# Node numbers in PSUM as bfloat16, written by a TensorE turn, for the 0/1 matrices of a graph layer

## What is computed

```python
h = (x_flat @ W_gat).reshape(M, HEADS, NUM_EXPERTS)
a_src = (h * att_src).sum(-1)
a_dst = (h * att_dst).sum(-1)
e = jax.nn.leaky_relu(a_src[src] + a_dst[dst], negative_slope=0.2)
e_max = jax.ops.segment_max(e, dst, num_segments=M)
ee = jnp.exp(e - e_max[dst])
denom = jax.ops.segment_sum(ee, dst, num_segments=M)
...
agg = jax.ops.segment_sum(msg, dst, num_segments=M).reshape(M, HEADS * NUM_EXPERTS) + b_gat
...
out = out + g[..., None] * (hh @ W2[ei] + b2[ei])
```

## Time and profile before

| | us |
|---|---|
| three runs: median (lowest to highest) | 1598.84 (1597.82 to 1599.68) |
| span of the profiled execution | 1598.4 |
| DVE busy | 1248.3 |
| POOL busy | 876.9 |
| PE busy | 869.5 |
| ACT busy | 451.1 |

### The profile page before, as it was taken

The page is one execution under the profiler, slowest core; times in us unless marked ns, Lnnn a source line. Parts: engine busy times, 40 slices in busy tenths (PEclk is TensorE's granted clock), DMA queues, the critical chain, the costliest instruction groups (busy, mean ns, idle before and its releaser), DMA issues.

```text
span 1598.4 us, 36932 instructions
## 1 busy us (share of the span) xinstructions
PE 869.5 (54%) x13361; PEld 683.8 (43%) x13361; DVE 1248.3 (78%) x2794; ACT 451.1 (28%) x813; POOL 876.9 (55%) x891
## 2 busy tenths in 40 slices
PE   0323233248888862554488884666666665553340
PEld 0223222237777752554133332555555555543340
DVE  6998898876667644996999986677777667788878
ACT  0232242224444433773133330212211121121120
POOL 0045665546666660000577777777777777777700
PEclk9999855556766655776699995555555555555555
DMA  7000000022222216100310110111111111111101
GB/s 166 7 20 21 27 28 27 29 56 50 51 49 49 50 51 95 42 28 12 29 10 10 10 10 10 12 12 12 12 14 12 13 12 12 12 12 24 23 2 26
DMA packets 113952, 45.80 MB, mean 29 GB/s; under 512 B 92631, under 2 KB 108799, under 8 KB 113538
## 3 DMA queue, kind: packets, MB, share of 16 engines
q1 hardware_dynamic: 84098, 22.43, 7.3%
q0 software_dynamic: 27632, 19.12, 7.0%
q10 hardware_dynamic: 2064, 2.10, 0.7%
HBM read 28.17 MB, written 15.93 MB: 28 GB/s over the span
## 4 chain that ended last, share of the span: by engine, by line
DVE 36%; issue 8%; PE 8%; DVEq 1%; ACT 0%; ACTq 0%
DVE edges_work L1950 7%; PE edges_acc L2460 3%; DVE edges_hotT L1950 3%; PE edges_acc L2449 2%; DVE all_stack L2195 1%; DVE graph_left L1823 1%; DVE graph_left L1821 1%; DVE all_eo L1992 1%; DVE all_sums L2211 1%; DVE edges_left L1821 1%; DVE edges_left L1823 1%; DVE graph_left L2274 1%; DVE edges_high L2244 1%; DVE all_sums L2271 1%; DVE edges_term_parts L1820 1%
## 5 line engine op out<-in xcount | busy, mean ns | idle before, releaser
L336 POOL DMA_INDIRECT edges_rows<-table,edges_src x576 | 563.0, 978 | 175.5 <-issue 174.9
L192 DVE TENSOR_TENSOR sorting_keys<-sorting_keys 128x512 f32<-128x512 f32 (+2 forms) x370 | 209.8, 608 | 16.6 <-ACT sorting_keys L317 13.2
L723 POOL DMA_INDIRECT x_rows<-mixture_sent,mixture_slot x128 | 144.3, 1128 | 127.5 <-DVE mixture_slot L785 89.0
L728 POOL DMA_INDIRECT y_rows<-mixture_yt,mixture_xin x144 | 156.2, 1085 | 103.6 <-ACT mixture_yt L950 79.4
L2508 ACT ACTIVATE edges_hotT<-edges_h 128x1024 bf16<-128x1024 bf16 x72 | 69.8, 1021 | 326.1 <-PE edges_h L2403 326.1
L1063 PE MATMUL mixture_bank<-mixture_xT,sorting_w_part 128*128 128x128 bf16 x864 | 111.9, 260 | 30.7 <-ACT mixture_xT L936 14.3
L1063 PEld LDWEIGHTS mixture_bank<-mixture_xT,sorting_w_part 128*128 x864 | 86.9, 107 | 57.4 <-issue 45.4
L1950 DVE TENSOR_TENSOR edges_work<-edges_feats,all_eo 128x2048 bf16<-128x2048 f32 x48 | 109.3, 2277 | 0.2 <-DVE all_eo L2003 0.2
L2460 PE MATMUL edges_acc<-edges_term_parts,edges_work 128*128 128x20 bf16 x1728 | 51.6, 179 | 100.6 <-DVE edges_term_parts L1824 100.6
L2460 PEld LDWEIGHTS edges_acc<-edges_term_parts,edges_work 128*128 128x128 bf16 x1728 | 49.1, 104 | 108.1 <-issue 108.1
L2403 PE MATMUL edges_h<-edges_ident,edges_work 128*128 128x128 bf16 x576 | 67.2, 310 | 31.7 <-DVE edges_work L1950 31.7
(11 more groups left out here) (477 smaller groups left out, 2170.0 us busy)
## 6 DMA issues: line engine op xcount, KB each, us to landing
edges_rows<-table,edges_src POOLq DMA_INDIRECT x576, 2.4
mixture_xin<-x_rows SPq DMA_DIRECT2D x144, 49.0 KB, 1.8
all_eo<-y_rows SPq DMA_DIRECT2D x16, 256.0 KB, 3.9
y_rows<-mixture_yt,mixture_xin POOLq DMA_INDIRECT x144, 2.6
sorting_w<-in_L_ffn_w_dram SPq DMA_DIRECT2D x4, 512.0 KB, 8.4
x_rows<-mixture_sent,mixture_slot POOLq DMA_INDIRECT x128, 2.3
out_dram<-all_x_sb SPq DMA_DIRECT2D x8, 256.0 KB
constants_src_i<-in_L_ffn_edge_index_dram SPq DMA_DIRECT2D x1, 1024.0 KB, 5.2
```

Of the source, the lines that this page charges most:

```text
L192: self.st.mark(dve.tensor_tensor(target[half], source[0], source[1], (ALU.min, ALU.max)[half]))
L336: pool.indirect_dma_start(to, None, rows, where).then_inc(done, 16)
L723: pool.indirect_dma_start(x_rows, bass.IndirectOffsetOnAxis(ap=slot[g % 2][:, c, t:t + 1], axis=0), now[c][:, t, :], None).then_inc(scatte ...
L728: pool.indirect_dma_start(y_rows, bass.IndirectOffsetOnAxis(ap=xin[j % XB][:, ROWX - 2:ROWX - 1].bitcast(U32), axis=0), yt[j % YB][:, :], ...
```

## The change

A third row of integers is written by POOL: `own_i`, in which every column of partition p holds p. DVE turns it to bfloat16 (`own16`). PE turns `own16` (a transpose with `ident16`) and writes the result as bfloat16 to 64 words of the bank of `node_ps`, beside the float32 numbers. The result is again the row 0 to 127 in each partition: `node_ps16`. The three calls of `equal_to` read `node_ps16` in place of `node_ps`; the float32 numbers stay for the stray edges. `ident16` is made earlier. PE waits for `own16` and `ident16`, and DVE waits for the turn before it writes `node_ps`.

```diff
+        own_i = a.sb("own_i", [P, P], I32)
+        own16 = a.sb("own16", [P, P], BF16)
...
+        node_ps16 = node_ps[:, P:P + P // 2].bitcast(BF16)
...
+        own_ready = a.sem("own_numbers_ready")
+        own_turned = a.sem("own_numbers_turned")
...
             pool.iota(node_i[:, :], pattern=[[1, P]], base=0, channel_multiplier=0).then_inc(numbered, 1)
+            pool.iota(own_i[:, :], pattern=[[0, P]], base=0, channel_multiplier=1).then_inc(numbered, 1)
...
-            spare = pool.alloc_register("pool_spare_edges"), numbered, 2
+            spare = pool.alloc_register("pool_spare_edges"), numbered, 3
...
-            dve.wait_ge(numbered, 2)
+            dve.wait_ge(numbered, 3)
             st.mark(dve.tensor_copy(block_f[:, :], part_i[:, :]))
+            st.mark(dve.tensor_copy(ident16[:, :], ident[:, :]))
+            st.link(dve.tensor_copy(own16[:, :], own_i[:, :]))
+            dve.sem_inc(own_ready, 1)
...
             def one_hot(s, u, g):
-                equal_to(hot[s % 4], node_ps, P, local16[:, u, tiles(g), :]).then_inc(hot_ready, 1)
+                equal_to(hot[s % 4], node_ps16, P, local16[:, u, tiles(g), :]).then_inc(hot_ready, 1)
...
-                equal_to(hot_last[at], node_ps, P, n16).then_inc(last_made, 1)
-                equal_to(hot_block[at], node_ps, T, b16).then_inc(last_ready, 1)
+                equal_to(hot_last[at], node_ps16, P, n16).then_inc(last_made, 1)
+                equal_to(hot_block[at], node_ps16, T, b16).then_inc(last_ready, 1)
...
-            st.mark(dve.tensor_copy(ident16[:, :], ident[:, :]))
             st.mark(dve.memset(one16[:, :], 1.0))
...
             st.link(dve.tensor_copy(node16[:, :], node_i[:, :]))
+            dve.wait_ge(own_turned, 1)
             st.mark(dve.tensor_copy(node_ps[:, 0:P], node16[:, :]))
...
             pe.wait_ge(node_steps, marks["feats"])
             turn_keys(0)
+            pe.wait_ge(own_ready, 1)
+            pe.transpose(node_ps16, own16[:, :], ident16[:, :]).then_inc(own_turned, 1)
             pe.wait_ge(at_ready, 2)
```

## The result

| | before | changed kernel |
|---|---|---|
| median of four runs each (lowest to highest), us | 1598.33 (1596.63 to 1599.68) | 1568.27 (1567.63 to 1570.0) |
| span of the profiled execution, us | 1598.4 | 1568.2 |
| DVE busy, us | 1248.3 | 1131.8 |
| POOL busy, us | 876.9 | 879.2 |
| PE busy, us | 869.5 | 861.8 |

The ratio is 0.9816, with a 95% interval of 0.9802 to 0.983: 30.1 us less. The prediction had 1568 and a range of 1564 to 1576. DVE was relieved of 1248.3 - 1131.8 = 116.5 us and the kernel became 30 us shorter; the difference is the subject of what follows.

The account below looks back on a forecast made before the run. DVE with its partners was taken to set the end, the gathers 31.0 us under it. 31.0 + 1.1 (last step's shorter begin) - 1.0 (longer gathers) = 31.1; span 1598.4 to 1567.3, plus 0.4, rounded to 1568 us; range 1564 to 1576.

Parts of the forecast that it names:

- The pace: DVE's comparison matrices: two elements per cycle with two-byte PSUM numbers, 2277 to 1210 ns for large, 1210 to 677 for small.
- Rival A: DVE's matrices: PSUM sets the pace, so they stay at 2277 ns and the time is 1599.2 us; 8 in 100.
- The start stage: Before the gathers: the new cast and wait make DVE's chain 0.35 us later; gathers still start at 775.0.
- The expert stage: DVE bounds it, PE would be next: a group falls from 11.11 to 9.96 us, 17.3 us over 15 groups.
- the late pairs: Two late pairs of matrices, on a chain of DVE and PE alone: 2 x 1.60 = 3.2 us gained.
- The edge steps: Each step gains 0.63 us, not 1.07, since DVE then waits for PE; 12.6 us up to step 20.
- Rival B: Edge steps: PE holds them and the earlier matrix gains nothing, 1577.6 us, or 1570 with a third; 8 in 100.
- The waits on gathers: DVE waits on gathers about 9 us at step 20 and some 3 us at the last step.
- The cap of 31.0: At the last step: gathers land 31.0 us before DVE begins it, so DVE's gain is cut to 31.0.
- longer gathers: Last lap: more of DVE's two-source work falls under the gathers and stretches some, an estimated loss of 1.0 us.
- Rival C: POOL's gathers: the faster form holds POOL one for one, adding 138 us, so 1706 us; 4 in 100.
- deciding point: Rival C decides the time from 31 us added to the gathers, 0.22 us for each us of matrices.

Follow-up runs that it names:

- experiment 4: Changed kernel, but each edge's number is read once with step 0 in the innermost dimension instead of from two copies side by side; 1598.66 us, ratio 1.0003.
- experiment 1: Changed kernel with all added parts kept, but the three `equal_to` calls read the float32 numbers; 1598.83 us, ratio 1.0 to the kernel before.
- experiment 10: The changed kernel again, unaltered, on the same chip as the others; 1569.71 us, ratio 0.9815 to the kernel before.
- experiment 2: Changed kernel, but the edge steps' matrices read the float32 numbers, so only the expert stage has the change; 1576.07 us, ratio 0.9857.
- experiment 3: Changed kernel, but the expert stage's matrices read the float32 numbers, so only the edge steps have the change; 1574.88 us, ratio 0.9851.
- experiment 6: Changed kernel with the last of the 16 gathers of each step left out, 36 of 576; 1550.85 us, ratio 0.971 to the kernel before.
- experiment 9: Changed kernel with the third set of source numbers placed at the second lap's last step, not its ninth (step 23, not 20); 1569.08 us, ratio 0.9814.
- experiment 8: Changed kernel with the start stage's second product made behind the table rows and the stray edges' gather issued after step 3's gathers; 1566.69 us, ratio 0.9805.
- experiment 11: Changed kernel with the edits of experiments 8 and 9 together; 1567.87 us, ratio 0.9807 to the kernel before.
- experiment 5: Changed kernel, but the three `equal_to` calls read the bfloat16 numbers in SBUF instead of PSUM; 1612.17 us, ratio 1.0093 to the kernel before.

## Why the prediction was right

**The pace.** 1210 and 677 ns were forecast; 1212 to 1217 and 678 were measured. Rival A, the old pace, is excluded for this form, and with it the rule of the Trainium skill's page "VectorE: DVE Perf Modes", section "The perf-mode tier table", that was cited for it: one element per cycle for any two-tensor operation with a PSUM operand. 2048 elements in 1212 ns contradict it. The prediction's own working rests on the width alone and has no term for the doubled copies of the edges' numbers; experiment 4 shows that without them the pace and the time of A come out.

**The start stage.** 0.35 us of cost was forecast. From the last copy of the rows for the table to the cast into PSUM, DVE took 6.38 us and now takes 6.70; experiments 1 and 10 have 6.71. Before, and then now:

```profile
763.64 0.29 DVE L1907 COPY edges_rows<-edges_as_sb 128x256 f32<-128x256 f32 x1
...
770.02 0.29 DVE L1982 CAST edges_feats<-edges_node 128x128 f32<-128x128 bf16 x1
```

```profile
762.74 0.29 DVE L1913 COPY edges_rows<-edges_as_sb 128x256 f32<-128x256 f32 x1
...
769.44 0.29 DVE L1991 CAST edges_feats<-edges_node 128x128 f32<-128x128 bf16 x1
```

That is 0.32 us. By the first matrix it is 0.6 (776.61 - 762.74 in place of 776.92 - 763.64), because two of DVE's operations beside the first gathers take 0.77 and 0.70 us where they took 0.56. The profiled execution also has all of the graph layer 0.9 us earlier (first gather at 774.1, has 775.0). This isn't the change's: the copy shown is already 0.9 us earlier, and it stands ahead of the first new instruction.

**The expert stage, a term sized too low.** 11.11 us per group were to become 9.96. Measured on one line of PE's timeline, the second layer of the networks:

```profile
851.20 1.07 PE L2328 MATMUL edges_acc<-edges_work,edges_u 128*64 128x512 f32 x2
...
861.12 1.07 PE L2328 MATMUL edges_acc<-edges_work,edges_u 128*64 128x512 f32 x2
```

It is 9.92 us. But the prediction counted the 15 groups behind the first and gave the first nothing. In the first group PE also waited for matrices: in the kernel before this line begins at 786.0 and begins for the last time at 956.5; in the changed kernel at 782.7 and 935.3. So 3.3 us are won as it begins, 0.9 of them the shift, and 21.2 at its end. Where 17.3 - 0.35 = 16.95 us were forecast, 20.3 came out: the first group's share was put at nothing without a reason. With the late pairs the first `raw` is at 975.77 and not 1001.46: 25.7 us, 24.8 without the shift, and 21.2 were forecast. Experiment 2 agrees: 22.5 us at the end, where the same terms of the prediction gave 20.2, its 1.07 for the first matrix of the edge steps left out.

**The edge steps.** 0.63 us per step were forecast. In the first lap the steps alternate between 13.28 and 13.54 us, a mean of 13.41, where before they were 14.03: 0.62. The wait of DVE for PE ahead of `found` came as described: 18.0 us over 36 steps, of which the last step has 1.6, as before. Rival B, no gain in the edge steps, is excluded by experiment 3 alone: 23.6 us.

**The waits on gathers.** Both stand where they were forecast. The one at step 20 is 13.0 us and not 9: the 3.6 us more that the expert stage gave are in it. The last one is 4.1 us and not 3: the last gather's rows came later than the sum had them. Experiments 2, 3, 6 and 9 show that these waits are the cap itself.

**The sum.** The cap of 31.0 less 1.0 for longer gathers puts DVE's last step at 1516.9; it begins at 1517.76, 0.8 us later. The last gather starts 0.3 us later than before though the first started 0.9 earlier, so the chain is 1.2 us longer, where 1.0 was estimated. And the last rows are there 3.9 us behind the start of the last gather, where the sum had the median landing of 2.4; in experiments 8 to 11 it is 2.6 to 3.7. The step's end then takes 1568.2 - 1517.8 = 50.4 us, as forecast; in experiments 2, 3 and 6, whose last step doesn't wait, it takes 51.5 as before. So the 3.6 us by which the expert stage was underrated don't show in the time: the cap absorbs them, and a forecast whose first term was off by a sixth still came out.

Part of the closeness is luck. The 1.0 us of longer gathers came out in size but not where it was looked for, in the last lap. The gathers of the two traces by the stretch in which they were issued, with POOL's time in them:

| | gathers | before, us | now, us |
|---|---|---|---|
| 950 to 1100 us, where the edge steps now begin earlier | 117 | 114.3 | 115.4 |
| 1300 to 1515 us, with the last lap | 163 | 165.7 | 166.0 |

The earlier start of 0.9 us, which isn't the change's, took back part of the late rows. And the span came out at 1568.2 where 1567.3 was forecast, while the median lies 0.1 above the span and not 0.4: a run's time is 1.8 us above its own span, and what lies between the median and the profiled span depends on which execution was profiled. Before it was rounded the forecast was 1567.7, 0.6 us off.

**Rival C.** Its mechanism is real, as experiment 5 shows, and for operands in SBUF it makes the kernel slower than before. With one operand in PSUM it isn't at work: the gathers keep their median of 944 ns, and the last starts 0.3 us later. The price in the rival, one for one, was three times too high: 0.32 us for each us of matrices. That is still above its deciding point of 0.22, and so the sign in experiment 5.

## What to carry to other kernels

When an engine on the bound gets faster work, first find the chain that runs beside it and how far ahead it ends: this distance, here 31 us of the 46 that DVE won, is about the most that can come out. A wait that appears behind such a change may be no new cost but the chain's own time, as both were here: moving one changed nothing (experiment 9), while the chain's count (experiment 6) and pace (experiment 5) changed the time. For small constant operands that are compared with two-byte data, it pays to try a two-byte copy in PSUM, with every operand advancing by one element, where POOL issues gathers meanwhile.

## What was not expected of the hardware

Two points were expected of the experiments but have no part in the prediction's sum. Two bytes in all three operands changed nothing as long as one was read with step 0 in the innermost dimension: 2283 ns, against 1217 with two copies side by side (experiment 4). And the same matrices at the same pace made the gathers' chain 44 us longer with the numbers in SBUF than with the numbers in PSUM (experiment 5); the size was not expected. Why a gather beside them is longer by 0.2 to 0.5 us and not by the whole matrix stays open; no run separates the parts of a gather. Where the last step waited for its rows, it began 2.5 to 3.9 us after the last gather's start (3.9 and 3.7 in two executions of the changed kernel, 2.5 to 2.8 in experiments 5, 8, 9 and 11), though the median landing is 2.4; what sets this wasn't tried.
